# The final part of a fused attention and mixture kernel: row sums moved to TensorE, weighting and normalisation to ScalarE, and GpSimd's power ahead of the row fetches

## The reference

```python
out = sum over experts e of cw[:, e] * (gelu(flat @ w1[e].T + b1[e]) @ w2[e].T + b2[e])
out = out.reshape(b, s, h) + hidden_states
mu, var = out.mean(-1), ((out - mu) ** 2).mean(-1)
g = (out - mu) * rsqrt(var + 1e-12) * ln_w + ln_b
x = x + s1 * g * sigmoid(g)
```

## Time and profile before

| | us |
|---|---|
| median of 3 runs (871.69 to 875.07) | 874.4 |
| the profiled execution's own time | 876.45 |
| its span in the profile | 874.6 |
| busy in the span: PE, DVE, ACT, POOL | 596.5, 660.3, 441.9, 436.9 |
| last DVE step of the final part: start, length | 871.20, 0.69 |

### The profile page before, as it was taken

The page is one execution under the profiler, slowest core; times in us unless marked ns, Lnnn a source line. Parts: engine busy times, 40 slices in busy tenths (PEclk is TensorE's granted clock), DMA queues, the critical chain, the costliest instruction groups (busy, mean ns, idle before and its releaser), DMA issues.

```text
span 874.6 us, 22303 instructions
## 1 busy us (share of the span) xinstructions
PE 596.5 (68%) x7049; PEld 402.2 (46%) x7049; DVE 660.3 (75%) x1711; ACT 441.9 (51%) x1075; POOL 436.9 (50%) x697
## 2 busy tenths in 40 slices
PE   1898899998988988842327777777777775324220
PEld 0566666665655655520214555555555553112110
DVE  4688888888787677743845898899898898617777
ACT  1456555554544454410417787888888774101111
POOL 3145555555457677657703344444444343764721
PEclk9999999998999799965658999999999997555555
DMA  9999999200000000001121232323232321111211
GB/s 228 345 283 287 286 288 287 75 0 0 0 8 18 15 18 18 16 13 45 48 76 38 85 99 93 102 81 104 85 100 85 96 69 41 52 45 36 66 31 36
DMA packets 127372, 80.93 MB, mean 93 GB/s; under 512 B 11832, under 2 KB 118208, under 8 KB 127296
## 3 DMA queue, kind: packets, MB, share of 16 engines
q1 hardware_dynamic: 122160, 70.97, 27.2%
q0 software_dynamic: 5136, 9.02, 3.8%
HBM read 18.85 MB, written 49.55 MB: 78 GB/s over the span
## 4 chain that ended last, share of the span: by engine, by line
PE 34%; DVE 33%; issue 17%; POOL 7%; ACT 4%; SPq 1%; DVEq 1%; DMA 1%; another core or an unknown queue 1%; POOLq 0%; ACTq 0%
PE m_ps L1047 5%; PE e_ps L1059 4%; DVE yts L1394 3%; POOL experts_sb L563 3%; DVE mneg L1142 3%; PE y_ps L1010 2%; PE q_ps L954 2%; PE m_ps L823 2%; PE p_ps L1003 2%; DVE pr L1391 2%; PE y_ps L887 2%; DVE pr L1393 2%; ACT pexp L610 2%; DVE rot L1184 2%; PE m_ps L837 2%
## 5 line engine op out<-in xcount | busy, mean ns | idle before, releaser
L610 ACT ACTIVATE pexp<-e_ps 128x512 f32<-128x512 f32 x128 | 76.5, 598 | 75.4 <-PE e_ps L870 66.7
L1142 DVE TENSOR_REDUCE mneg<-m_ps 128x4 bf16<-128x512 f32 x128 | 84.7, 683 | 22.5 <-PE m_ps L837 22.2
L1047 PE MATMUL m_ps<-xs,wb 128*128 128x512 f16 x276 | 80.4, 403 | 19.8 <-issue 18.6
L563 POOL DMA_INDIRECT experts_sb<-ybuf,slots x64 | 63.5, 993 | 32.3 <-issue 18.9
L492 POOL DMA_INDIRECT xbuf<-x,slots x64 | 65.2, 1019 | 16.6 <-issue 14.9
L1019 PE MATMUL p_ps<-eye_sb,yn 128*128 128x128 f32 x32 | 11.6, 363 | 80.4 <-DVE yn L1399 64.2
L887 PE MATMUL y_ps<-pexp,vd 128*32 128x128 f32 x512 | 57.6, 295 | 3.1 <-ACT pexp L610 1.0
L557 POOL TENSOR_TENSOR pexp<-rot,pexp 128x512 f16<-128x512 f32 x24 | 27.8, 1157 | 56.6 <-ACT pexp L731 56.6
L851 PE MATMUL e_ps<-early 128*128 128x256 bf16 x256 | 52.0, 284 | 0.1
L557 POOL TENSOR_TENSOR pexp<-qt,pexp 128x512 f16<-128x512 f32 x24 | 30.3, 1264 | 43.1 <-ACT pexp L731 43.1
L1101 PE MATMUL e_ps<-b_sb,cwt 8*128 8x128 f32 x64 | 16.6, 436 | 49.3 <-ACT cwt L780 49.3
(11 more groups left out here) (223 smaller groups left out, 2129.7 us busy)
## 6 DMA issues: line engine op xcount, KB each, us to landing
xbuf<-zero_sb SPq DMA_DIRECT2D x71, 256.0 KB, 4.0
ybuf<-zero_sb SPq DMA_DIRECT2D x71, 256.0 KB, 3.6
wb<-experts_sb SPq DMA_DIRECT2D x46, 256.0 KB, 2.3
xs<-xbuf SPq DMA_DIRECT2D x23, 256.0 KB, 2.7
ybuf<-vd SPq DMA_DIRECT2D x23, 256.0 KB, 2.2
experts_sb<-in_experts_w SPq DMA_DIRECT2D x8, 512.0 KB, 6.9
x_all<-in_x SPq DMA_DIRECT2D x8, 256.0 KB, 5.3
xbuf<-x,slots POOLq DMA_INDIRECT x64
```

Of the source, the lines that this page charges most:

```text
L563: nc.gpsimd.indirect_dma_start(yg[:, 2 * (B * n + b) + k, :], None, ybuf, bass.IndirectOffsetOnAxis(ap=slots[:, k, B * n + b:B * n + b + 1 ...
L610: nc.scalar.activation(pexp[:, j, :, :], e_ps[j % 2][:, :, :], ACT.Exp, scale=float(D) ** -0.5).then_inc(exp_ready.sem, 1)
L1047: last = nc.tensor.matmul(u_ps[f % 2], wb1[:, i % 2, f, a, :], xg16[:, i % 2, b, :], start=k == 0, stop=k == len(PARTS) - 1)
L1142: nc.vector.tensor_reduce(mneg[:, n.batch, j // 2, (j % 2) * NG:(j % 2) * NG + NG], m_ps[j % 2][:, :, :], AX.X, ALU.max, negate=True).then ...
```

## The change

Adding up a round moves to PE, as products with the identity matrix that accumulate in the PSUM bank which holds the bias product: one for the residual (in `bias_terms`) and one for each of the two experts of a token (`mix`). The weights per token are multiplied in place by ACT (`weigh_rows`) before that; the layout of `yg` changes so that the four tiles of one expert choice lie side by side. ACT also normalises (`normalise`), with a scale and an offset per token, which reads the bank and writes `y2`. DVE keeps the statistics (`spread`), adds epsilon, forms the offset (`offset`), and gates. POOL keeps the power alone (`inverse_root`), fetches two rounds at the start instead of five, and fetches round n + 2 behind the power of round n. `y2` gets a second buffer in place of the two accumulators.

```diff
-GATE = 5
+GATE = 4
...
-                for b in range(B):
-                    for k in range(2):
-                        nc.gpsimd.indirect_dma_start(yg[:, 2 * (B * n + b) + k, :], None, ybuf,
+                for k in range(2):
+                    for b in range(B):
+                        nc.gpsimd.indirect_dma_start(yg[:, (2 * n + k) * B + b, :], None, ybuf,
                                                      bass.IndirectOffsetOnAxis(ap=slots[:, k, B * n + b:B * n + b + 1], axis=0)).then_inc(s_gathered[n], 16)
 
-            def deviation(n):
-
-                pool.wait_ge(s_spread, B * (n + 1))
-                nc.gpsimd.tensor_tensor(rstd2[:, n % 2, 0, :], mv2[:, n % 2, :, 1], eps2_sb[:, :], ALU.add).then_inc(s_rstd2, 1)
-                pool.wait_ge(s_rstd2, 2 * n + 1)
-                nc.gpsimd.tensor_tensor(rstd2[:, n % 2, 1, :], rstd2[:, n % 2, 0, :], half_sb[:, 0:1].to_broadcast([P, B]), ALU.pow).then_inc(s_rstd2, 1)
+            def inverse_root(n):
+
+                pool.wait_ge(s_rstd2, 3 * n + 1)
+                nc.gpsimd.tensor_tensor(rstd2[:, n % 2, 0, :], rstd2[:, n % 2, 0, :], half_sb[:, 0:1].to_broadcast([P, B]), ALU.pow).then_inc(s_rstd2, 1)
...
-            for n in range(5):
-                gather(n)
+            gather(0)
+            gather(1)
             for n in range(TAUS):
-                deviation(n)
-                if n + 5 < TAUS:
-                    gather(n + 5)
+                inverse_root(n)
+                if n + 2 < TAUS:
+                    gather(n + 2)
...
             def cw_copy(n):
 
                 act.wait_ge(s_cw_transposed, n + 1)
-                after(act, s_bias_summed, n - 1)
+                after(act, s_mixed, n - 1)
                 nc.scalar.copy(cwt[:, n % 2, :, :], m_ps[n % 2][0:E, :, :]).then_inc(s_cw_copied, 1)
+
+            def weigh_rows(n):
+
+                act.wait_ge(s_gathered[n], 16 * 2 * B)
+                for k in range(2):
+                    for b in range(B):
+                        t = B * n + b
+                        last = nc.scalar.mul(yg[:, (2 * n + k) * B + b, :], yg[:, (2 * n + k) * B + b, :], rs[:, 7 - k, t:t + 1])
+                    last.then_inc(s_weighed, 1)
+
+            def normalise(n):
+
+                act.wait_ge(s_rstd2, 3 * n + 3)
+                after(act, s_result, n - 1)
+                for b in range(B):
+                    last = nc.scalar.activation(y2[n % 2][:, b, :], d_ps[n % 2][:, b, :], ACT.Identity,
+                                                scale=rstd2[:, n % 2, 0, b:b + 1], bias=rstd2[:, n % 2, 1, b:b + 1])
+                last.then_inc(s_normed2, 1)
+
+            def tangent(n):
+
+                act.wait_ge(s_gate, GATE * n + 2)
+                nc.scalar.activation(e2, y2[n % 2], ACT.Tanh, scale=0.5).then_inc(s_tanh, 1)
 
             cw_copy(0)
             cw_copy(1)
+            weigh_rows(0)
             for n in range(TAUS):
-                act.wait_ge(s_gate, GATE * n + 3)
-                nc.scalar.activation(e2, y2, ACT.Tanh, scale=0.5).then_inc(s_tanh, 1)
+                if n:
+                    tangent(n - 1)
+                normalise(n)
                 if n + 2 < TAUS:
                     cw_copy(n + 2)
+                if n + 1 < TAUS:
+                    weigh_rows(n + 1)
+            tangent(TAUS - 1)
...
                 pe.wait_ge(s_cw_copied, n + 1)
-                after(pe, s_biased, n - 1)
+                after(pe, s_normed2, n - 1)
                 for b in range(B):
-                    last = nc.tensor.matmul(d_ps[n % 2][:, b, :], cwt[:, n % 2, b, :], b2_sb[:, :], start=True, stop=True)
-                last.then_inc(s_bias_summed, 1)
+                    nc.tensor.matmul(d_ps[n % 2][:, b, :], cwt[:, n % 2, b, :], b2_sb[:, :], start=b == 0, stop=False, skip_group_check=True)
+                nc.tensor.matmul(d_ps[n % 2], eye_sb[:, :], xn1_all[:, B * n:B * n + B, :], start=False, stop=False, skip_group_check=True)
+
+            def mix(n):
+
+                for k in range(2):
+                    pe.wait_ge(s_weighed, 2 * n + k + 1)
+                    last = nc.tensor.matmul(d_ps[n % 2], eye_sb[:, :], yg[:, (2 * n + k) * B:(2 * n + k) * B + B, :], start=False, stop=k == 1,
+                                            skip_group_check=True)
+                last.then_inc(s_mixed, 1)
 
             pe.wait_ge(s_gelu, 2 * FB * PASSES)
             pe.wait_ge(s_y_copied, PASSES)
+            bias_terms(0)
             for n in range(TAUS):
-                bias_terms(n)
+                if n + 1 < TAUS:
+                    bias_terms(n + 1)
+                mix(n)
...
-            def combine(n):
-
-                a, m = acc[n % 2], mv2[:, n % 2, :, :]
-                dve.wait_ge(s_bias_summed, n + 1)
-                nc.vector.tensor_tensor(a, xn1_all[:, B * n:B * n + B, :], d_ps[n % 2], ALU.add).then_inc(s_biased, 1)
-                dve.wait_ge(s_biased, n + 1)
-                dve.wait_ge(s_gathered[n], 16 * 2 * B)
-                for k in range(2):
-                    for b in range(B):
-                        t = B * n + b
-                        if k:
-                            dve.wait_ge(s_mixed, 2 * B * n + b + 1)
-                        nc.vector.scalar_tensor_tensor(a[:, b, :], yg[:, 2 * t + k, :], rs[:, 7 - k, t:t + 1], a[:, b, :],
-                                                       ALU.mult, ALU.add).then_inc(s_mixed, 1)
+            def spread(n):
+
+                m = mv2[:, n % 2, :, :]
+                dve.wait_ge(s_mixed, n + 1)
                 for b in range(B):
-                    dve.wait_ge(s_mixed, 2 * B * n + B + b + 1)
-                    nc.vector.bn_stats(stats2[:, b, :], a[:, b, :]).then_inc(s_stats2, 1)
+                    nc.vector.bn_stats(stats2[:, b, :], d_ps[n % 2][:, b, :]).then_inc(s_stats2, 1)
                 for b in range(B):
                     dve.wait_ge(s_stats2, B * n + b + 1)
                     nc.vector.bn_aggr(m[:, b, :], stats2[:, b, :]).then_inc(s_spread, 1)
+                dve.wait_ge(s_spread, B * (n + 1))
+                after(dve, s_normed2, n - 1)
+                nc.vector.tensor_scalar(rstd2[:, n % 2, 0, :], m[:, :, 1], 1e-12, None, ALU.add).then_inc(s_rstd2, 1)
+
+            def offset(n):
+
+                dve.wait_ge(s_rstd2, 3 * n + 2)
+                nc.vector.scalar_tensor_tensor(rstd2[:, n % 2, 1, :], mv2[:, n % 2, :, 0], -1.0, rstd2[:, n % 2, 0, :],
+                                               ALU.mult, ALU.mult).then_inc(s_rstd2, 1)
...
-                a, m, r = acc[n % 2], mv2[:, n % 2, :, :], res[n % 2]
-                dve.wait_ge(s_rstd2, 2 * n + 2)
-                for b in range(B):
-                    last = nc.vector.tensor_scalar(y2[:, b, :], a[:, b, :], m[:, b, 0:1], rstd2[:, n % 2, 1, b:b + 1], ALU.subtract, ALU.mult)
-                done(last)
-                done(nc.vector.tensor_tensor(y2[:, :, :], y2[:, :, :], lnw_sb[:, :].unsqueeze(1).to_broadcast([P, B, C]), ALU.mult))
-                done(nc.vector.tensor_tensor(y2[:, :, :], y2[:, :, :], lnb_sb[:, :].unsqueeze(1).to_broadcast([P, B, C]), ALU.add))
+                y, r = y2[n % 2], res[n % 2]
+                dve.wait_ge(s_normed2, n + 1)
+                done(nc.vector.tensor_tensor(y, y, lnw_sb[:, :].unsqueeze(1).to_broadcast([P, B, C]), ALU.mult))
+                done(nc.vector.tensor_tensor(y, y, lnb_sb[:, :].unsqueeze(1).to_broadcast([P, B, C]), ALU.add))
                 after(dve, s_out[n % 2], 16 * (n // 2))
-                done(nc.vector.tensor_tensor(r, y2[:, :, :], s1_all[:, B * n:B * n + B, :], ALU.mult))
+                done(nc.vector.tensor_tensor(r, y, s1_all[:, B * n:B * n + B, :], ALU.mult))
                 dve.wait_ge(s_tanh, n + 1)
...
             for n in range(TAUS):
-                combine(n)
+                spread(n)
                 if n:
                     gate(n - 1)
+                offset(n)
             gate(TAUS - 1)
```

More of the change, by code:

```diff
@@ L230, in program @@
         rstd2 = sb("rstd2", [P, 2, 2, B])
-        eps2_sb = sb("eps2_sb", [P, B])
         m_ps = [bank(f"m_ps{i}", [P, NG, P]) for i in range(2)]
@@ L245, in program @@
         last_sb = early[:, 0:2 * ORD * SW].rearrange("p (b w) -> p b w", b=2)
-        y2, e2, res0, acc0 = (xs[:, i, :, :, :].rearrange("p h s d -> p (h s d)").bitcast(F32).rearrange("p (b c) -> p b c", b=B)
+        y2, e2, res0, y3 = (xs[:, i, :, :, :].rearrange("p h s d -> p (h s d)").bitcast(F32).rearrange("p (b c) -> p b c", b=B)
                               for i in range(4))
@@ L261, in program @@
         w16 = experts_sb[:, :, :].bitcast(F16).rearrange("p k (s c) -> p k s c", s=2)
-        res1, acc1 = (gel[i].rearrange("p (b c) -> p b c", b=B) for i in range(2))
-        res, acc = [res0, res1], [acc0, acc1]
+        res1 = gel[0].rearrange("p (b c) -> p b c", b=B)
+        res, y2 = [res0, res1], [y2, y3]
         yg = experts_sb
@@ L373, in program @@
         s_outs = sem("s_outs")
-        s_biased = sem("s_biased")
```

(3 more changed lines are left out.)

## The result

The changed kernel takes 890.22 us (median of 4 runs, 885.73 to 890.63) where the kernel before takes 874.74 in the same comparison: a ratio of 1.0168, 95% interval 1.0123 to 1.0213, so 15.5 us slower. The forecast was slower, by 9.4. A second comparison later gave 887.91 against 876.51 (1.0151, 1.0105 to 1.0196); one of the 13 runs of the kernel before there took 1783.88 us and is left out as a slow one. The profiled execution took 890.63, its span is 888.8; against the span of 874.6 of the kernel before that is 14.2 more.

What follows compares the result with a forecast made beforehand. A ring of waits through DVE, ACT and PE bound a round (9.7 us), with DVE busiest. Afterwards 783.2 + 11.6 + 66.5 + 11.3 + 8.7 + 2.7 = 884.0 against a span of 874.6, 9.4 more; range 869 to 899.

Steps and rivals of the forecast that it cites:

- The late handovers: From about 756 us, engines start late on finished results beside 40 unbroken fetches; removing them brings the out projection 15.8 us forward.
- Last out projection: PE's last out projection before the final rounds, forecast at 768.7 us where it stood at 784.48.
- First power: POOL's first power, forecast at 783.2 us (before 796.13), including 2.0 us saved by bursts at the higher clock.
- First to second power: Time between POOL's first two powers, with no gate in it: 11.6 us set by POOL, 10.8 on the ring.
- the ring: Cycle of waits through DVE, ACT and PE that sets a round: 14.4 us at 1.2 GHz, 13.3 with the clock's help.
- The turns: Five rounds between the second power and the last turn, forecast at 13.3 us each, 66.5 together.
- the three products: PE's identity products of 512 float32 columns per round: 1.71 us each at 1.2 GHz, 5.34 together with 0.21 ending.
- The risk named at the end of the prediction: PE's 512-column products had no row in this stage's trace; 0.3 us more each would add 1 us a turn.
- Last turn and end: Turn to the last power, without copy and bias, 11.3 us; then 8.7 for the last gates and 2.7 to the end.
- rival 1: PE's clock stays at 2.4 GHz, POOL bounds turns at 11.6 us, total 869.4 on the median; chance 0.14.
- come back in the rounds: Rival: late handovers stay at the start (15.8 us more, 899.6) or return in the rounds, 2 or 3 us each; chance 0.16.
- The wash: Rival: turns of 11.8 to 12.5 us, so the start pays for the rounds; 872 to 878 in all; chance 0.20.

Runs made afterwards that it cites:

- the higher level: Comparisons in which the unedited kernel before took 874.4 to 876.5 us, as in most of the comparisons.
- the run with a busy PE: Changed kernel plus five unread 512-column products on PE in each of rounds 2 to 7: 872.70 us, ratio 1.0165 at the lower level.
- variant with both moves: Changed kernel, offset and normalisation ahead of the previous round's gate, PE's bias and residual products directly before their own round's sums: 868.27 us, ratio 1.0129.
- the lower level: The one comparison of four edited kernels in which the unedited kernel before took 857.74 us, 17 less than in all others.

## Why the prediction was right, and where its size was off

- *Start.* The late handovers went as forecast, and the run with five rounds at the start brought them back. Last out projection 770.38 against 768.7 forecast, of which 0.9 is that the first fetch itself was later (733.54 against 732.60); from there to the first power 13.4 us against 14.5, as the clock helped more: the second burst ran at 2.4 GHz throughout (bias products 1.15 at 778.28, both sums 1.88 at 780.33). First power 783.79 against 783.2. One sign named in the prediction was wrong: it asked for no idle time of over 3 us on DVE between 756 and 784, and there are two, 4.22 and 12.85 us. Its own sum has them, since DVE must wait for PE's next sums and later for the first round's products.
- *First to second power.* 12.26 against 11.6. I let POOL bound it; the ring did, 1.2 us of POOL's idle time ahead of the second power show it. My 10.8 for the ring was too low: this burst ran at 1.2 GHz to its end (two sums in 3.62 us), and the rest is in the next point.
- *The turns* are the mis-sized term of the sum: 14.48, 14.08, 13.85, 13.77, 13.70 us, 69.9 in all, where five of 13.3 make 66.5: 3.4 of the 4.8 us by which the span (888.8) exceeds the sum (884.0). In the turn of the chain, forecast and measured (each from its start there to the next one's): statistics 1.26 and 1.37; gate 3.65 and 3.50; offset 0.24 and 0.11; **normalisation 1.0 and 1.50** (no row stood behind the 1.0; 0.36 us lie between the first of its four and the second); copy 0.57 and 0.49; bias 2.0 and 2.07; **the three products** 5.34 at 1.2 GHz, less 1.1 for the clock, and 4.72. A product costs 1.87 us at 1.2 GHz, not the 1.71 that I scaled from 432 columns, so the three would be 5.8; the clock gave 1.1 back in this turn, as forecast for each, and less in the ones before it, since the raised clock only reached the end of the burst: the two sums took 3.60 us in the turn of 14.48 and 2.83 in that of 13.70. The risk named at the end of the prediction, dearer products of 512 columns, came in at 0.16 instead of 0.3 each.
- *Last turn and end.* 11.51 against 11.3, and 11.36 from the last power to the span's end against 11.4.
- *Who waits.* Offset directly behind the gate, DVE waiting 8.8 to 9.5 us a turn for PE (I said some 7), POOL idle 1.2 to 2.8 before its power (1.5), clock 0.63 (0.6 to 0.7).
- *Luck.* The forecast holds for the higher level, at which the change gains 12.3 us at the start. See the last point for the lower one.
- *Rivals.* The clock did not rise for good; the run with a busy PE shows that it could have, and that it would have been worth 11 us, with POOL then bounding the turn as rival 1 said. The late handovers did not come back in the rounds: DVE's statistics start at the end of PE's sums. The wash, at 12.4 us a turn, was 1.6 us short of the mean turn.
- *Still open.* What makes the handovers late is not shown beyond its condition: a train of 40 fetches on end does it at the higher level, trains of 16 and of 8 never did, 24 did not in the one comparison where it was tried. Also open is why the kernel before was 17 us faster in that comparison, on the same chip as the comparison before it, in which it took 875.06. Since the changed kernel seems to have nothing to gain from the start there, it would lose more: its variant with both moves was 1.3% slower, and by F (155.3 against 138.8) the unedited one would take some 16 us more than that variant, so some 27 us more than the kernel before, nearly three times the forecast; worked out, not measured.

## What to carry to other kernels

Relieving the busiest engine is worth nothing if the moved work is put in a ring: before moving, write down for each wait what stands ahead of the instruction that ends it, on every engine; here one move (bias and residual products beside their own round) was worth 15 us with no work saved. Work given to PE in bursts with pauses between them may run mostly at 1.2 GHz, as it did here with 7 us of work and 6.6 of pause, so cost it at that clock, or keep PE at work in between. And a deep prefetch issued in one go can cost more than it hides, as the 40 fetches did here (63.5 us to the first power against 45.6 with 16): fetch in parts, and give each round no more than the ring has room for.

## What the runs showed of the hardware that was not expected

- A train of 40 indirect fetches from POOL makes handovers between PE, DVE and ACT late by up to 11 us (PE's first bias product, 790.02 us in the changed kernel with five rounds at the start, behind 11.83 us of idle time where the unedited one has 0.66), 17.0 us in all at the first power; 32 fetches in parts of 16, 8 and 8 do not. At the lower level 24 in one go do not either. The mechanism is open.
- A product of the identity with 512 float32 columns takes 1.87 us from start to start at 1.2 GHz and 0.94 to 0.96 at 2.4 GHz, which is 3.65 and 1.85 ns a column; 432 columns of another product took 3.33 a column at 1.2 GHz.
- Adding 4.5 us of useless products a round to PE shortened the final part by 11 us (F 143.9 against 155.3), with nothing else changed; the mean granted clock went from 0.63 to 0.93.
- Of four activations of 128 columns from PSUM with a scale and a bias per row, the second starts 0.36 us behind the first; the four take 1.50.
- POOL's power takes 1.38 to 1.53 us in most places beside DVE's gate steps, though 1.04 at two (824.28 and 847.82 us, PE kept busy) and 1.26 at one (812.27 us, five rounds at the start), and 1.01 to 1.05 where DVE stands still; in the kernel before it also takes 1.01 to 1.05 beside DVE's weighted sums and normalisation.
